# Second attention on 32-row and 32-column tiles of PE, conditioning weights rounded by ACT in the first attention

## The chip, the cores and the metric

One Trainium2 chip, one of its cores, one launch. The metric is the device time of one execution in microseconds. The core has five engines that run beside each other, each in its own program order, and wait for each other at semaphores: PE multiplies matrices, DVE (VectorE) and ACT (ScalarE) work element by element and read PE's results from PSUM (eight banks of 128 x 512 fp32), POOL (GpSimd) works on SBUF alone, SP issues transfers.

## The reference, cut to what matters

Four transformer blocks in a row on x of 4 batches x 256 tokens x 128 features, with a conditioning vector per batch:

```python
# layer 0: 16 heads of 64, then an MLP with gelu
qkv = mod(layernorm(x)) @ W_qkv; x += g1 * (softmax(q k^T / 8) v @ W_out + b_out); x += g2 * mlp(...)
# layer 1: rms norm modulated by a small net, rotary embedding, 16 heads of 8, gated MLP
n = ada_rmsnorm(x, c, w_norm1, t1_w1, ...); q, k = rope(n @ wq + bq), rope(n @ wk + bk)
x += softmax(q k^T / sqrt(8)) v @ wo + bo;  x += (gelu(n2 @ w_gate) * (n2 @ w_up)) @ w_down
# layer 2: every linear layer rounds its rows to 8 bits and its weights to -1, 0, 1
def weight_quant(w): s = 1 / clip(mean(|w|), 1e-5); return clip(round(w * s), -1, 1) / s
h = bitlinear(silu(c), wa0); h = hgrn_mlp(h, wa1, wa2); h = bitlinear(h, wa3) + ba3
params = bitlinear(rmsnorm(h) * wr, wa4) + ba4            # shift, scale, gate for the tokens
x = ...  (products with wi, wf, wg, wo, wm1, wm2 and a recurrent scan)
# layer 3: linear attention with 16 heads of 8
```

The change concerns the attention of layer 1 (the second attention) and the conditioning chain of layer 2, which depends on the condition alone: wa0, wa1, wa2, wa3, wa4 ("the conditioning layers").

## The kernel before, in words

Everything stays in SBUF. Tokens lie in eight tiles of 128; banks, semaphores and the order of each engine's instructions are written out by hand, so an engine waits wherever its next instruction waits, with all that is queued behind it.

*First attention* (layer 0): 32 pairs of heads, one pair a round. PE makes the scores of two heads on two 64-row tiles (`pair_scores`), projects queries, keys and values of the next batch (`unit`), transposes the normalised probabilities of the pair two rounds back (`turn0`) and multiplies the values of the pair three rounds back on two 64-column tiles (`pair_values`). DVE takes maxima (`top0`) and copies transposed probabilities (`take0`), ACT makes exponentials with their sums, POOL multiplies by the reciprocals.

Then ACT sums the absolute weights of wa4 (`weight_sums`), the small products for layer 1's and layer 3's scales follow, and layer 0's MLP. The other sums are made by ACT between its steps up to the start of the second attention. POOL rounds all of layer 2's weights during the second attention and after it (`whole_weights`), three steps for each.

*Preparation of layer 1:* products with Wqkv, rotation by DVE, then queries and keys are split into a high and a low part so that fp32r products stay exact: a head of 8 features has 32 rows of `qaT` and `kaT` (high, low, high, low against high, high, low, low). Four heads lie in the 128 rows of one group.

*Second attention:* 64 heads (4 batches x 16), one a round, in the loop `for i in range(NH + 3)`. Since four heads share the 128 rows, the keys of one head are copied into a buffer `kaM` that is zero in the other 96 rows (`masked_key`), by DVE for the first 16 and by ACT for the rest. In a round PE makes two score matmuls (`scores`), transposes the probabilities of the head two rounds back in four 128 x 128 pieces (`turn`), and multiplies the values of the head three rounds back in four matmuls of 96 columns (`values`; the trace records each fp32 matmul as two passes, so eight rows a head; fp32r matmuls and transposes are one pass each). DVE reduces the maxima of the head (`top`) and copies the transposed probabilities (`take`); every fourth round it normalises (`normalise`). ACT makes two exponentials of 128 x 256 with the maximum as bias, each with its sum.

The conditioning layers are woven into this loop (`weave`): each begins at the round that `WEAVE` gives it and takes one step a round: square (ACT), power (POOL), products and maxima of a row (DVE), rounding, transposes (PE), product (PE), result (ACT).

## Time and profile before

| | |
|---|---|
| median of 3 runs | 538.32 us (538.28 to 545.02) |
| the profiled execution | 538.68 us |
| its span | 536.9 us, 8122 instructions |
| busy: PE, DVE, ACT, POOL | 412.2, 370.8, 306.4, 193.6 us |
| mean granted clock of PE | 0.869 of full speed |

The span runs from the first to the last instruction of the profiled execution. An engine's busy time counts every moment in which one of its instructions runs. A row of the chain of waits names the work that the end of the kernel depended on at that moment. Times below are counted from the start of the span. The page cuts the span into 40 slices; PE's clock in tenths is 9 (full) in most of the first 28 and 5 in most of the last 12.

### The profile page before, as it was taken

To read this page: it belongs to the slowest core of one execution; us is meant where nothing else is said; L and a number is where in the kernel's file an instruction comes from. 1 tells how busy PE (TensorE), PEld (TensorE's weight loads), DVE (VectorE), ACT (ScalarE), POOL (GpSimd) and SP (SyncE) were. 2 spreads that over 40 slices of the span, in tenths; PEclk is the share of its full clock that TensorE was granted. 3 is DMA by queue.
4 is the path that set the end of the run, shared out by engine and by line. 5 is a ranking of instruction groups with operands and counts; after the bars stand their busy time and mean duration, and the time that the engine had idled before them with its cause. 6 is when DMAs were issued, how large, how long until landed. Compare 5 with 4: busy or idle time off the path is not lost.

```text
span 536.9 us, 8122 instructions
## 1 busy us (share of the span) xinstructions
PE 412.2 (77%) x2641; PEld 310.5 (58%) x2641; DVE 370.8 (69%) x904; ACT 306.4 (57%) x957; POOL 193.6 (36%) x189
## 2 busy tenths in 40 slices
PE   5989999999999678757898999899992531155564
PEld 5656566667576556447797899888451421004353
DVE  4456557557579334967996788877369459879794
ACT  1574654653666384686689788555731861275352
POOL 1043434433466220015585855300673022272101
PEclk9999999999999969797999799899997555555597
DMA  8930000000000000000000000000000000000001
GB/s 319 444 153 1 1 1 1 1 2 2 0 3 1 1 0 2 0 0 2 1 2 0 2 2 1 1 2 1 0 1 0 1 0 0 0 2 1 0 2 39
DMA packets 3842, 13.33 MB, mean 25 GB/s; under 512 B 372, under 2 KB 2420, under 8 KB 3284
## 3 DMA queue, kind: packets, MB, share of 16 engines
q1 hardware_dynamic: 3800, 12.80, 6.0%
q8 instruction: 22, 0.36, 0.3%
q14 instruction: 20, 0.16, 0.1%
HBM read 12.28 MB, written 0.52 MB: 24 GB/s over the span
## 4 chain that ended last, share of the span: by engine, by line
PE 54%; DVE 23%; ACT 9%; issue 7%; POOL 5%; DMA 1%; POOLq 0%; SPq 0%; ACTq 0%; DVEq 0%
PE bank L927 6%; PE bank L884 6%; PE bank L907 6%; PE bank L954 6%; PE bank L941 5%; PE bank L912 3%; DVE area L1313 3%; PE bank L870 3%; PE bank L969 3%; ACT tab_ L487 3%; DVE area L1316 2%; DVE tab_ L1313 2%; PE bank L861 2%; ACT big L487 2%; PE bank L1021 2%
## 5 line engine op out<-in xcount | busy, mean ns | idle before, releaser
L487 ACT ACTIVATE tab_<-bank,nmax 128x256 f32<-128x256 f32 x168 | 77.6, 468 | 40.6 <-DVE nmax L1457 31.5
L884 PE MATMUL bank<-vpad,xT 128*128 128x96 f32 x512 | 71.2, 285 | 6.6 <-DVE xT L1463 6.4
L884 PEld LDWEIGHTS bank<-vpad,xT 128*128 128x128 f32 x512 | 65.7, 201 | 10.1 <-DVE xT L1463 9.3
L487 ACT ACTIVATE area<-bank 128x512 f32<-128x512 f32 (+3 forms) x68 | 36.9, 549 | 56.9 <-PE bank L912 19.9
L396 POOL TENSOR_TENSOR big<-big,rrec 128x512 f32<-128x512 f32 x44 | 44.8, 1040 | 66.0 <-DVE rrec L1507 65.9
L1491 DVE TENSOR_REDUCE nmax<-bank 128x2 f32<-128x512 f32 x64 | 43.2, 677 | 32.0 <-PE bank L927 32.0
L1499 DVE COPY area<-bank 128x512 f32<-128x512 f32 x64 | 42.5, 684 | 14.6 <-PE bank L941 13.4
L1457 DVE TENSOR_REDUCE nmax<-bank 128x2 f32<-128x512 f32 x64 | 43.6, 681 | 11.8 <-PE bank L861 11.4
L487 ACT ACTIVATE big<-bank,nmax 128x256 f32<-128x256 f32 x88 | 40.6, 472 | 17.9 <-PE bank L907 10.6
L1463 DVE COPY xT<-bank 128x512 f32<-128x512 f32 x64 | 43.4, 678 | 1.9 <-PE bank L870 1.5
L870 PE MATMUL bank<-tabs,tab_ 128*128 128x128 f32 x256 | 41.1, 286 | 0.0
L861 PE MATMUL bank<-kaM,qaT 128*128 128x256 f32 x128 | 32.8, 340 | 6.9 <-ACT tab_ L487 5.6
L907 PE MATMUL bank<-xT,w0s 128*128 128x256 f32 x128 | 33.9, 396 | 4.4 <-issue 4.4
L927 PE MATMUL bank<-area 64*128 64x256 f32 x256 | 36.3, 402 | 0.0
L1182 PE MATMUL bank<-identb,area 128*128 128x128 bf16 x40 | 6.0, 310 | 38.1 <-DVE area L1316 38.0
L954 PE MATMUL bank<-area 128*64 128x256 f32 x256 | 34.7, 392 | 0.6 <-ACT big L487 0.6
L424 POOL TENSOR_SCALAR area<-area 128x4 f32<-128x4 f32 x14 | 3.9, 276 | 85.9 <-ACT tab_ L487 54.8
L487 ACT ACTIVATION_READ_ACCUMULATOR tab_<-bank,nmax 128x1 f32 x168 | 33.1, 197 | 0.0
L442 POOL TENSOR_SCALAR w2s<-w2s 128x768 f32<-128x768 f32 (+4 forms) x15 | 32.5, 2169 | 1.2
L487 ACT ACTIVATE big<-bank 128x256 f32<-128x256 f32 (+1 forms) x41 | 17.7, 434 | 25.2 <-PE bank L954 16.3
L870 PEld LDWEIGHTS bank<-tabs,tab_ 128*128 128x128 f32 x256 | 31.6, 147 | 0.0
L927 PEld LDWEIGHTS bank<-area 64*128 64x128 f32 x256 | 22.0, 186 | 14.2 <-issue 12.8
(224 smaller groups left out, 909.4 us busy)
## 6 DMA issues: line engine op xcount, KB each, us to landing
w2s<-w SPq DMA_DIRECT2D x1, 4352.0 KB, 26.8
rows<-row SPq DMA_DIRECT2D x1, 1600.0 KB, 10.9
w0s<-w SPq DMA_DIRECT2D x3, 512.0 KB, 6.8
w1s<-w SPq DMA_DIRECT2D x1, 1408.0 KB, 15.8
w0s<-w SPq DMA_DIRECT2D x1, 1024.0 KB, 12.9
xs<-x SPq DMA_DIRECT2D x1, 512.0 KB, 4.3
out<-tab_ SPq DMA_DIRECT2D x2, 256.0 KB, 2.3
tabs<-tab SPq DMA_DIRECT2D x1, 421.5 KB, 5.2
```

Source lines behind the costliest of these rows:

```text
L396: pool.tensor_tensor(prob[n % SLOTS], prob[n % SLOTS], rrec0[:, n % 4, :].unsqueeze(2).to_broadcast([P, QT, SEQ]), ALU.mult).then_inc(S("a ...
L487: return nc.scalar.activation(o, i, f, **kw)
L861: m = mm(bank[half][:, q * SEQ:(q + 1) * SEQ], queries(q), keys, start=True, stop=True)
L870: m = nc.tensor.transpose(bank[2 + half][:, k * SEQ + q * P:k * SEQ + (q + 1) * P], A.prob[:, slot, q, k * P:(k + 1) * P], ident)
L884: m = mm(bank[4 + gslot][:, o:o + v(k).shape[1]], A.pT[:, half, k, q * P:(q + 1) * P], v(k), start=(k == 0), stop=(k == QT - 1))
L907: m = mm(to[:, cc * SEQ:(cc + 1) * SEQ], part(w0s, W0, "qkv", at, at + P), rhs, start=True, stop=True)
L927: m = mm(bank[(2 * p + a) % 4][:, q * SEQ:(q + 1) * SEQ], qT[r, b % 2, c, q * P:(q + 1) * P], kT[r, b % 2, c, :], start=True, stop=True)
L954: m = mm(bank[6][a * DH0:(a + 1) * DH0, 0:SEQ], vs[:, b % 2, k, c * P + a * DH0:c * P + (a + 1) * DH0], pT[:, (2 * p + a) % 4, k, :], star ...
L1457: V.tensor_reduce(nmax[:, half, :], bank[half][:, :].rearrange("p (q k) -> p q k", q=QT), AX, ALU.max, negate=True).then_inc(S(A.tag + "_m ...
L1463: V.tensor_copy(A.pT[:, half, :, :].rearrange("p k q -> p (k q)"), bank[2 + half][:, :]).then_inc(S(A.tag + "_pT"), 1)
L1491: V.tensor_reduce(nmax0[:, n % 4, :], bank[n % 4][:, :].rearrange("p (q k) -> p q k", q=QT), AX, ALU.max, negate=True).then_inc(S("a0_max" ...
L1499: V.tensor_copy(pT[:, n % 4].rearrange("p k q -> p (k q)"), bank[4 + n % 2][:, :]).then_inc(S("a0_pT"), 1)
```

## The change

*Second attention.* The zero-padded key copies, the transposes of the probabilities, their copies and the sums in ACT go. The scores are now computed twice, in two orientations, both on 32-row tiles: once with queries along the partitions, only for the maxima (`scores1`), and once with keys along the partitions (`shifted_scores`), so that the exponential is written in the orientation that the value product needs. Two heads are worked on at a time, in the order 0, 2, 4, 6, 1, 3, 5, 7 of eight, so that the two lie in different row tiles. The maxima of eight heads are split into a high and a low part (`maxima`, DVE), turned by PE, copied by ACT and added to the second scores by a matmul with a selecting matrix `picks`. The exponential is one activation of 512 a head. The values are padded to 32 columns with a one behind the eight features, so that one product gives values and sums; four heads go to four 32-column tiles of one bank (`values1`). They come out with features along the partitions and are turned back once a batch (`turn_values`), then normalised.

Scores run 12 rounds ahead of their second computation (`LEAD`), the values lag 18, and the loop has 90 rounds, two at a time. Four banks are a ring that scores, maxima, turned values and the conditioning products enter in one fixed order; three banks hold the second scores, one the values.

*Weights.* The absolute sums are made by DVE in rounds 5 to 11 of the first attention, added up by one matmul in round 12, and the conditioning weights are rounded by ACT in 20 pieces in rounds 14 to 27 (`rounds` and `signs`: scale and add a large number, then the sign of what is left), in place. POOL rounds only layer 2's token weights, between the steps of the conditioning layers. POOL's clearing of the value buffer waits for the last normed batch of the first attention. A result of the conditioning layers is taken one round earlier (RESULT 9 becomes 8).

```diff
-            def core_exp(A, n, slot, half, gslot, hg, g=None):
-                act.wait_ge(S(A.tag + "_max"), n + 1)
-                act.wait_ge(S(A.tag + "_T"), n + 1)
-                for q in range(QT):
-                    e = acti(A.prob[:, slot, q, :], bank[half][:, q * SEQ:(q + 1) * SEQ], ACT.Exp,
-                             bias=nmax[:, half, q:q + 1], accum_out=rsum[:, gslot, q, hg:hg + 1])
+            def exponents1(n):
+                act.wait_ge(S("a1_Z"), n + 1)
+                if n >= 8:
+                    act.wait_ge(S("a1_PV"), (n - 8) // 4 + 1)
+                acti(pT1[:, n % 8].rearrange("p k q -> p (k q)"), bank[4 + n % 3][:, :], ACT.Exp
+                     ).then_inc(S("a1_exp"), 1)
...
+            def scores1(n):
+                to = [ring_enter("S", x, 0) for x in (n, n + 1)]
+                for q in range(QT):
+                    for x in (n, n + 1):
+                        r, g, at = group_of(x)
+                        m = mm(to[x - n][:, q * SEQ:(q + 1) * SEQ], qaT[r, g, at + q * P:at + (q + 1) * P],
+                               kaT[r, g, at:at + SEQ], start=True, stop=True)
...
+            def shifted_scores(n):
+                if n % 8 == 0:
+                    pe.wait_ge(S("a1_M"), n // 8 + 1)
+                if n >= 2:
+                    pe.wait_ge(S("a1_exp"), n - 1)
+                for x in (n, n + 1):
+                    r, g, at = group_of(x)
+                    mm(bank[4 + x % 3][:, :].rearrange("p (k q) -> p k q", k=QT), picks[r, g, :],
+                       mrow[r, x // 8 % 2, :].unsqueeze(1).to_broadcast([32, QT, SEQ]), start=True, stop=False)
+                for k in range(QT):
+                    for x in (n, n + 1):
+                        r, g, at = group_of(x)
+                        m = mm(bank[4 + x % 3][:, k * SEQ:(k + 1) * SEQ], kaT[r, g, at + k * P:at + (k + 1) * P],
+                               qaT[r, g, at:at + SEQ], start=False, stop=(k == QT - 1))
+            def values1(u, k):
...
+                for n in range(4 * u, 4 * u + 4):
+                    h = head_of(n)
+                    j, low = h % 8 // 2, h % 2
+                    at = 16 + ((b * QT + k) * H + h) * 32 - 16 * low
+                    m = mm(bank[7][32 * j:32 * j + 32, part_ * SEQ:(part_ + 1) * SEQ], vpad[:, at:at + 32],
+                           pT1[:, n % 8, k, :], start=(low == 0 and k == 0), stop=(low == 1 and k == QT - 1))
...
+            for i in range(0, ROUNDS, 2):
                 if i < NH:
+                    scores1(i)
+                if i % 8 == M_LAG % 8 and 0 <= i - M_LAG < NH:
+                    turn_maxima((i - M_LAG) // 8)
...
                 weave(i)
+                weave(i + 1)
+                if 0 <= i - PV_LAG < NH:
+                    values1((i - PV_LAG) // 4, (i - PV_LAG) // 2 % 2)
+                if LEAD <= i < NH + LEAD:
+                    shifted_scores(i - LEAD)
...
-                acti(into[0:r, 0:src.shape[1]], src, ACT.Abs, accum_out=wsum[0:r, j:j + 1]).then_inc(S("wsum"), 1)
+                acti(rounded_at[u % 2][0:r, 0:n], src, ACT.Identity, scale=wscale[0:r, j:j + 1], bias=magic[0:r, 0:1]
+                     ).then_inc(S("wq_round"), 1)
...
+                acti((wa2q if name == "wa2" else w2q)[:, 2 * (lo + (0 if name == "wa2" else W2[name][0])):][:, 0:n],
+                     rounded_at[u % 2][0:r, 0:n], ACT.Sign, bias=magic[0:r, 1:2]).then_inc(S("wq"), 1)
...
-            pool.memset(kaM[:, :, :].bitcast(F32), 0.0).then_inc(S("kaM_zero"), 1)
+            pool.wait_ge(S("a0_normed"), NB)
+            pool.memset(vpad[:, :], 0.0).then_inc(S("v_zero"), 1)
```

PE in the middle of the second attention, three heads before (names: `bank` is PSUM, then the two operands):

```order
L861 MATMUL bank<-kaM,qaT 128x256 x2
L870 MATMUL bank<-tabs,tab_ 128x128 x4
L884 MATMUL bank<-vpad,xT 128x96 x4
L861 MATMUL bank<-kaM,qaT 128x256 x2
L870 MATMUL bank<-tabs,tab_ 128x128 x4
L884 MATMUL bank<-vpad,xT 128x96 x4
```

and in the changed kernel at the same place, where the rows from one L1157 to the next are two heads:

```order
L1157 MATMUL bank<-kaT,qaT 128x256 x4
L1199 MATMUL bank<-big,vpad 32x256 x4
L1178 MATMUL bank<-mrow,picks 128x512 x2
L1183 MATMUL bank<-qaT,kaT 128x256 x4
L1157 MATMUL bank<-kaT,qaT 128x256 x4
L1167 MATMUL bank<-tabs,w0s 128x128 x2
L1199 MATMUL bank<-big,vpad 32x256 x4
L1178 MATMUL bank<-mrow,picks 128x512 x2
```

Two heads are 14 instructions where they were 20, and none of them is a transpose, apart from the two for the maxima of eight heads (L1167).

DVE at the first step of the third conditioning layer before, where L1457 is the reduction of the maxima and L1463 the copy of the transposed probabilities:

```order
L1457 TENSOR_REDUCE nmax<-bank 128x2
L1463 COPY xT<-bank 128x512
L1313 TENSOR_TENSOR big<-big 4x576
L1457 TENSOR_REDUCE nmax<-bank 128x2
L1463 COPY xT<-bank 128x512
L1668 SCALAR_TENSOR_TENSOR big<-big,a4s,adrs 4x576
```

and now:

```order
L1561 TENSOR_REDUCE nmax<-bank 128x2 x2
L1414 TENSOR_TENSOR w0s<-w0s 4x576
L1561 TENSOR_REDUCE nmax<-bank 128x2
L1810 SCALAR_TENSOR_TENSOR w0s<-w0s,a4s,adrs 4x576
L1561 TENSOR_REDUCE nmax<-bank 128x2
```

The copies are gone and the conditioning steps stand among half as many operations as before.

ACT in round 15 of the first attention, where it gets two pieces of weights; before:

```order
L487 ACTIVATE area<-bank 128x512
L487 ACTIVATE big,rsum<-bank,nmax 128x256 x4
L487 ACTIVATE big<-bank 128x256
```

and now:

```order
L531 ACTIVATE area<-bank 128x512
L531 ACTIVATE big,rsum<-bank,nmax 128x256 x2
L531 ACTIVATE tab_<-w2s,magic,wscale 128x384 x2
L531 ACTIVATE big,rsum<-bank,nmax 128x256 x2
L531 ACTIVATE w2s<-tab_,magic 128x384 x2
L531 ACTIVATE big<-bank 128x256
```

Four activations stand between and behind the exponentials of the pair.

## Rows read from the trace of the kernel before

**Rows 1.** The page, part 4: the chain that ended last, by engine.

```profile
PE 54%; DVE 23%; ACT 9%; issue 7%; POOL 5%; DMA 1%; POOLq 0%; SPq 0%; ACTq 0%; DVEq 0%
```

**Rows 2.** Stages: length, busy us of each engine (instructions), PE clock, DMA.

```profile
14.00:173.00 159.00, 151.25 (x978) 101.79 (x976) 100.03 (x201) 90.15 (x314) 63.18 (x64) 1.00 0.12 50
...
254.00:372.00 118.00, 110.21 (x879) 102.89 (x880) 98.20 (x220) 85.68 (x297) 57.68 (x41) 0.96 0.01 1
...
440.00:505.00 65.00, 20.87 (x109) 10.41 (x110) 57.36 (x171) 26.53 (x82) 24.61 (x30) 0.50 0.00 1
```

**Rows 3.** The same view, the second attention and its first stretch at half clock.

```profile
239.10:374.10 135.00, 121.59 (x947) 113.55 (x947) 112.15 (x245) 97.49 (x335) 64.67 (x45) 0.94 0.01 1
...
242.40:249.20 6.80, 6.03 (x28) 5.97 (x29) 4.45 (x9) 5.55 (x23) 2.27 (x4) 0.50 0.01 4
```

**Rows 4.** Timeline (start us, us, what, idle before): both ends of the second attention.

```profile
237.98 1.09 ACT L487 ACTIVATE kaT<-bank 128x512 fp32r<-128x512 f32 x2 [0.32 <-PE bank L1065]
...
374.12 0.66 PE L1103 MATMUL bank<-tabs,xn 128*128 128x128 f32 x4 [0.63 <-DVE xn L1313]
```

**Rows 5.** Chain of waits in order of time (start, us): one head.

```profile
280.65 0.27 PE bank L861 x2
280.91 0.44 PE bank L870 x4
281.35 0.87 PE bank L884 x8
```

**Rows 6.** Chain of waits, first attention: 16 fp32 matmuls (32 passes) of 256 columns.

```profile
14.50 7.14 PE bank L907 x32
```

**Rows 7.** Timeline of PE, first attention: one round with no projections.

```profile
145.66 1.14 PE L927 MATMUL bank<-area 64*128 64x256 f32 x8
...
146.72 1.09 PE L941 MATMUL bank<-tabs,big 128*128 128x128 f32 x8
...
147.75 1.08 PE L954 MATMUL bank<-area 128*64 128x256 f32 x8
```

**Rows 8.** Groups of DVE, 239.1 to 374.1 us (busy us, mean ns, idle before).

```profile
L1457 DVE TENSOR_REDUCE nmax<-bank 128x2 f32<-128x512 f32 x64 | 43.6, 681 | 11.8 <-PE bank L861 11.4
...
L1463 DVE COPY xT<-bank 128x512 f32<-128x512 f32 x64 | 43.4, 678 | 1.9 <-PE bank L870 1.5
...
L1641 DVE CAST kaM<-kaT 32x256 fp32r<-32x256 f32 x16 | 8.3, 520 | 4.2 <-ACT kaT L487 3.7
...
L1313 DVE TENSOR_TENSOR xn<-bank,rrec 128x32 f32<-128x32 f32 x32 | 4.6, 185 | 0.5
```

**Rows 9.** Groups of ACT in the same stretch.

```profile
L487 ACT ACTIVATE tab_<-bank,nmax 128x256 f32<-128x256 f32 x128 | 59.2, 466 | 32.0 <-DVE nmax L1457 31.5
...
L487 ACT ACTIVATE kaM<-kaT 32x256 fp32r<-32x256 f32 x48 | 19.7, 410 | 0.9
...
L487 ACT ACTIVATE big<-bank,a4s 4x384 f32<-4x384 f32 x5 | 2.8, 568 | 0.1
...
L487 ACT ACTIVATE big<-bank 128x512 f32<-128x512 f32 x1 | 0.6, 593 | 0.0
```

**Rows 10.** Stages, columns as in rows 2: rounds 15 and 24 of the first attention.

```profile
99.79:103.80 4.01, 4.01 (x29) 2.40 (x28) 2.64 (x5) 2.69 (x13) 2.04 (x2) 1.00 0.01 2
...
145.70:148.80 3.10, 3.10 (x28) 2.03 (x26) 1.98 (x5) 2.12 (x10) 1.13 (x3) 1.00 0.00 0
```

**Rows 11.** Timeline between the attentions.

```profile
184.93 4.04 ACT L487 ACTIVATE big<-w2s 128x4608 bf16<-128x4608 f32 x1 [4.03 <-PE bank L969]
...
188.01 3.69 DVE L1316 TENSOR_SCALAR xn<-xs,mv,rstd 128x128 f32<-128x128 f32 x2 [0.81 <-POOL rstd L402]
...
188.04 3.51 POOL L411 MEMSET kaM<- 128x4096 f32 x1
...
193.43 1.95 PE L852 MATMUL bank<-tabs,xn 128*128 128x128 f32 x8
...
195.69 6.54 PE L1030 MATMUL bank<-xT,w0s 128*128 128x512 f32 x12 [0.32 <-ACT xT L487]
```

More of the change, by code:

```diff
@@ L557, in _ @@
                     exponents(2 * s)
+                for u in pieces_of(s):
+                    rounds(u)
                 for i in units[1:2]:
@@ L561, in _ @@
                     exponents(2 * s + 1)
+                for u in pieces_of(s):
+                    signs(u)
                 for i in units[2:]:
```

475 lines of the change are left out of this document (279 added, 196 removed).

## The prediction

> **What bounds the kernel now.** I read the chain of waits first. It gives PE 54% of the span and DVE 23% [rows 1], so I went on to the stages. In the first attention PE is busy 151.3 of 159.0 us at the full clock; in the second it is busy 110.2 of 118.0 us at a granted clock of 0.96, and DVE is busy 98.2 us of the same stretch [rows 2]. The whole second attention, from the last piece of the transposed keys at 239.1 us to the turn of its last outputs at 374.1 us, takes 135.0 us [rows 3, 4]. That is a quarter of the kernel, and nearly all of the change lies in it.
>
> What sets that stage is PE's work for one head. In a run without stalls the eight value passes take 0.87 us (four fp32 matmuls, each recorded as two passes), the two scores 0.27 and the four transposes 0.44, together 1.58 us [rows 5]. Sixty-four heads are 101 us of the 135. The other 34 are the start, the conditioning products woven in, waits of the three engines for each other, and stretches at half clock, of which the first runs from 242.4 to 249.2 us [rows 3]. A change that only shortened one of DVE's or ACT's operations would be hidden here; this one takes away PE work.
>
> **The second attention, change part by part.** The sum is made against the profiled execution, 538.7 us (span 536.9), which is 0.4 us above the median of 538.32.
>
> *PE.* Transposes (4 a head) go, and so do the value matmuls that load 128x128 weights for 96 columns. A pair of heads now costs four score matmuls, two of 512 columns that add the maxima, four transposed scores, and four fp32 value matmuls of 32 output partitions. Prices: an fp32r matmul of 256 columns is one pass and costs 0.135 us (two in 0.27 [rows 5]); an fp32 one is two passes of 0.223, 0.45 us alone (16 matmuls, 32 passes, in 7.14 [rows 6]); two on 64-row tiles or on 64-column tiles cost what one costs, since eight passes start-to-start take 1.06 and 1.01 us and not 1.78 [rows 7]. Loads of weights share in no row: eight 128-column ones take 0.87 us, 0.109 each [rows 5]. The trace has no 32-row or 32-column tile. Bounds for the ten fp32r matmuls of a pair: all in twos, 0.81; ten weight loads one after another, 1.09; no sharing, 1.62. I take 1.2, near the middle one, because the 64-row tiles share and the loads don't. Values: 0.45 us if four column tiles run together, 0.89 if two do, as now, 1.78 if none does; I take 0.5. Each round changes between kinds of tile twice. Eight 64-row passes as four pairs would be 4 x 0.223 = 0.89 and take 1.06 [rows 7], so a change costs about 0.17 us, two 0.34. Sum: 2.04 us, against 3.16 now. The turns of maxima (two transposes and a change for eight heads) and of values, and the woven products (25 passes and 15 small transposes, some 7 us), add about 0.36 a pair: **2.4 us.**
>
> The Trainium skill speaks against this layout on one point: "TensorEngine Tiling (Array Packing)", section Key Properties, says that changing the tiling mode drains TensorE. The trace agrees, the 0.17 us above being what such a change costs here. Without it the pair would be 2.06 us, with it 2.4.
>
> *DVE.* It keeps one reduction a head and loses the copy of the turned probabilities (43.4 us), the key casts (8.3 us) and most of the normalising [rows 8]. Durations overlap a little: DVE was busy 112.2 us [rows 3] while the rows of the stage add up to about 122, so I scale by 0.91: 0.62 us a reduction. The conditioning layers' small operations are what is left of the 112.2 after the two big groups, the casts, the normalising, its 16 reciprocals of 0.19 and the residual (2 x 0.69): about 17 us. They stay. New: eight times two small operations for the maxima (0.2 us each, like the 128x32 ones [rows 8], 3 us), four normalisings of about 0.6 us (2.4). So from the thirteenth head on DVE owes per pair 1.24 + 22.4/26 = 2.1 us. **PE stays the bound, with DVE close behind.**
>
> *ACT.* Two exponentials of 256 with accumulated sums and a key copy of 0.41 (mean, 48 of them) become one exponential of 512. An evacuation of 512 from PSUM is 0.593 us [rows 9], so a pair is 1.1 to 1.2 us. ACT is not the bound.
>
> *The stage in rounds.* The program runs the exponential 12 heads behind the scores, so there is a head and a tail. Rounds 0 to 11, reductions only: 12 x 0.62 and 1.1 for the first maxima and the first score, 8.5 us. Rounds 12 to 63: 26 pairs x 2.4 = 62.5 us. Rounds 64 to 75, no reductions left: six pairs, each of which waits on three banks. PE may write a pair only after the exponential two heads back, so a period is PE's six matmuls (0.65 to 0.8), two hand-overs (0.3) and one exponential (0.6), 1.65 us, 10 us in all. Last values, copy, four transposes, normalising: 3.5 us. That is 84.5 us without waits. Before, waits, weaving, cold clock and start made 34 us over PE's per-head work. The weaving and the start are in my sum already and POOL has less to do between two steps of a conditioning layer, so I take 8 of the 34. The stage becomes **92.5 us, 42.5 us less**. The bounds of this term are 0 and 34 us: 84.5 and 118.5.
>
> **The other stages.** *First attention, +3 us.* DVE gets 14 sums of weights in rounds 5 to 11 (0.2 to 1.3 us by their width), where PE needs more than twice the time of these sums for its own round; that is hidden. ACT gets 20 pieces of two activations of 384. A 384-wide one with a pointer scale on 4 rows is 0.568 us [rows 9]; two with overlap are about 1.07 us. In round 15 ACT is busy 2.69 of 4.01 us [rows 10] and gets two pieces, 4.8 us: 0.8 too much. Round 24 has 2.12 of 3.10 and gets one, 3.2: 0.1 too much; six or seven rounds are like these two, most others have room. Taken together 1.5 to 2 us, and as much again for exponentials that come later to POOL. Bounds 0 and 8 us. If the cover in rounds 14 to 27 were gone altogether the 20 pieces would cost 21 us.
>
> *Between the attentions, -5 us.* ACT's sum of 4608 weights (4.04 us) stood ahead of the table load and the small conditioning matmuls, so PE turned the normed rows only at 193.43 [rows 11]. Now those matmuls follow the first attention directly and are done near 187. What is late next is DVE's normed batch: its two operations took 3.69 us because POOL's memset of 3.51 us ran beside them [rows 11]. POOL now waits for that batch before it clears the value buffer, so the batch ends near 188.5 and the first hidden layer starts near 190.1 instead of 195.69. The memset then runs beside the small operations that make the scales, and PE's fifth hidden matmul waits for these. I take 5 of the 5.6 us; bounds 3 and 7, the upper one if the clock no longer falls. The Trainium skill names such a mechanism ("GPSIMD Engine Reference", section Key points: GpSimd shares its SBUF interfaces with VectorE); the row with 3.69 us agrees.
>
> *Preparation and tail, -0.5.* One more DVE operation (a cast of 512 elements, 0.5 to 1 us) stands ahead of the DVE-bound rotation; the three key casts ahead of the first score go, 0.5 us. POOL's rounding of weights behind the second attention delayed nothing but some 0.5 us.
>
> 538.7 + 3 - 5 - 42.5 - 0.5 = 493.7, or 493.3 on the scale of the median: **493 us**.
>
> **Rivals.**
> 1. *The three engines keep waiting for each other as before.* Rounds are shorter, but a conditioning layer still needs eight hand-overs, two table switches and POOL's power, and ring banks used for its products make the next scores wait for ACT. Then the stage is 118.5 us and the time 519. For it: the 34 us of today. Against it: POOL's 768-wide roundings are gone.
> 2. *Column tiles run by twos at most*, as in the rows. A pair is 0.39 dearer: 8.5 + 26 x 2.8 + 12 + 3.5 + 8 = 105, time 506. For it: [rows 7] show two. Against it: nothing there says that two is the limit.
> 3. *Half clock through the stage.* Two of four row groups work at a time. The last stages run at 0.50 with PE busy 20.9 of 65.0 us [rows 2]. PE's passes double and a pair is 4.4: 8.5 + 114 + 19 + 4 + 6 = 152, time 553. Against it: PE's queue would hardly be idle, and the stages with PE busy over 90% had 0.96 and 1.00.
> 4. *Slower than before: 32-wide tiles do not run side by side at all.* A pair is 1.62 + 1.78 + 0.34 + 0.36 = 4.1 us, the drain 3.6 a pair: 8.5 + 107 + 22 + 3.5 + 8 = 149, time 550. The point from which it decides, for this and for rival 3, is about 3.7 us a pair (26 of them and six of the drain at 0.5 less, with 20 us of ends and waits, fill the 137.5 us that would cancel the other gains). For it: no row has such tiles. Against it: both 64-wide kinds share.
> 5. *Row tiles share their loads too.* Then PE owes 0.81 + 0.5 + 0.34 + 0.36 = 2.0 and DVE's 2.1 is the bound: 8.5 + 55 + 10 + 3.5 + 2 = 79, time 480; with the best bounds elsewhere 475.
>
> **How the numbers follow.** Chances: forecast (483 to 503) 0.56, rival 1 0.10, rival 2 0.14, rival 3 0.06, rival 4 0.04, rival 5 0.10. A change under 2% (10.8 us) cannot be told from none; that limit is 527.6. The forecast and rivals 1, 2 and 5 lie clear of it: 0.89 faster. Cases between rival 1 and rivals 3 and 4 give 0.03 within; slower 0.08. The range runs from 476 to 519: it takes in rival 2, nearly all of rival 5 and half of rival 1.
>
> **What the next profile would show.** Right: about 92 us from the last key copy to the last turn; PE busy over 90% of it, most idle time of the 64 reductions put down to its scores; the first hidden layer near 190 us plus what the first attention grew; 32-row matmuls starting in twos a few ns apart. Wrong if: four 32-column passes take 0.45 us (rival 2) or 0.9 (4), the granted clock of the stage is under 0.7 (3), PE is idle over 20 us of it (1), or the rounds 15 to 27 of the first attention are 1 us longer each.

## The result, and the profile after

The changed kernel takes 521.5 us (median of 4 runs, 517.8 to 525.6) against 538.4 of the kernel before in the same job: 0.961 of it, 95% interval 0.953 to 0.969. It is faster by 17 us where 45 were forecast, and lies outside my range (476 to 519). The profiled execution took 520.65 us, its span is 518.9. Run again later, the same kernel took 529.0 us (520.7 to 532.1), 0.972 of before (0.961 to 0.983). A kernel's profile is that of its first run, which was among the slower ones of e4, e7, e13 and e16 below and the fastest of e6.

Part 2 of its page, the row of PE's clock (40 slices of the span, tenths of full speed), and part 4, the chain by engine:

```profile
PEclk9999999999999989877575555997895555555597
PE 57%; DVE 25%; ACT 7%; issue 7%; POOL 2%; DMA 1%; POOLq 0%; SPq 0%; ACTq 0%; DVEq 0%
```

Before, the clock was nearly all 9 up to slice 28. Now it is at 5 in slices 18 to 25, which is the second attention. The view by stretches says the same in numbers; its columns are those of [rows 2]:

```profile
14.00:172.50 158.50, 149.65 (x962) 100.82 (x962) 109.03 (x214) 108.79 (x349) 62.18 (x62) 1.00 0.12 50
238.50:352.00 113.50, 84.58 (x663) 47.87 (x663) 62.19 (x141) 53.74 (x112) 23.96 (x32) 0.65 0.00 1
238.50:248.80 10.30, 4.79 (x30) 3.12 (x30) 9.09 (x23) 2.59 (x7) 3.99 (x8) 0.64 0.00 0
248.80:336.80 88.00, 68.89 (x521) 39.06 (x521) 50.48 (x113) 41.63 (x83) 19.28 (x22) 0.60 0.00 1
268.90:327.00 58.10, 46.06 (x319) 25.46 (x317) 32.71 (x72) 21.67 (x46) 15.39 (x14) 0.50 0.00 1
327.00:352.00 25.00, 18.41 (x198) 9.95 (x190) 8.28 (x17) 15.15 (x35) 0.69 (x2) 1.00 0.00 1
336.80:348.20 11.40, 8.77 (x90) 4.45 (x90) 1.84 (x4) 7.75 (x15) 0.00 (x0) 1.00 0.01 1
352.00:372.00 20.00, 20.00 (x52) 10.28 (x51) 5.19 (x13) 10.85 (x26) 1.76 (x3) 0.74 0.00 1
```

The second row is the whole second attention. The turn of its last outputs starts at 351.60 us, 0.4 before the end of the row, so in the measure of [rows 3] and of my forecast (from the end of the last key copy to that start) it takes 113.1 us where it was 135.0 and where I had 92.5. The granted clock is 0.65 where it was 0.94, and for 58 us on end it is at the lower of its two levels. PE is idle for 28.9 of the 113.5 us. The third, fourth and seventh rows are rounds 0 to 11, 12 to 63 and 64 to 75. I had 8.5, 62.5 and 10 us for them, and 8 us of waits: nearly all of the miss is in the 88.0.

PE's timeline, one pair of heads at full and one at half clock (start, us, what, idle before):

```profile
262.21 0.50 PE L1178 MATMUL bank<-mrow,picks 32*128 32x512 f32 x2
262.55 0.39 PE L1183 MATMUL bank<-qaT,kaT 32*128 32x256 f32 x4
262.78 0.40 PE L1157 MATMUL bank<-kaT,qaT 32*128 32x256 f32 x4
263.11 0.64 PE L1199 MATMUL bank<-big,vpad 128*32 128x256 f32 x8
263.80 0.50 PE L1178 MATMUL bank<-mrow,picks 32*128 32x512 f32 x2
...
286.42 0.79 PE L1178 MATMUL bank<-mrow,picks 32*128 32x512 f32 x2
287.01 0.63 PE L1183 MATMUL bank<-qaT,kaT 32*128 32x256 f32 x4
287.45 0.62 PE L1157 MATMUL bank<-kaT,qaT 32*128 32x256 f32 x4
288.00 1.08 PE L1199 MATMUL bank<-big,vpad 128*32 128x256 f32 x8
289.01 0.79 PE L1178 MATMUL bank<-mrow,picks 32*128 32x512 f32 x2
```

From one L1178 to the next, a pair is 1.59 us at full clock and 2.59 at half. Every other pair is shorter where nothing is woven in. In these the first scores of a later pair (L1157) lie in the other two row tiles and start 0.02 us behind the selecting matmuls (L1178); from the L1178 to the next it is 1.43 us at full clock (333.99 to 335.42) and 2.16 at half:

```profile
302.63 0.79 PE L1178 MATMUL bank<-mrow,picks 32*128 32x512 f32 x2
302.65 0.79 PE L1157 MATMUL bank<-kaT,qaT 32*128 32x256 f32 x4
303.22 0.62 PE L1183 MATMUL bank<-qaT,kaT 32*128 32x256 f32 x4
303.77 1.08 PE L1199 MATMUL bank<-big,vpad 128*32 128x256 f32 x8
304.79 0.79 PE L1178 MATMUL bank<-mrow,picks 32*128 32x512 f32 x2
```

The answer to [rows 5] is a full-clock run of value passes in the chain, 16 passes in four column tiles:

```profile
348.24 1.11 PE bank L1199 x16
```

Who waited for whom in 238.5 to 352 us (us, times, longest):

```profile
ACT big L531 <- PE bank L1183: 48.6, 28, 5.8
DVE nmax L1561 <- PE bank L1157: 36.9, 16, 5.9
...
PE bank L1107 <- DVE w0s L1417: 8.5, 5, 3.5
...
PE bank L1210 <- ACT xT L531: 5.4, 4, 2.2
```

DVE and ACT wait for PE, and PE waits for DVE's clipped rows of a conditioning layer at its transposes (L1107), and for the copy of the values. The timeline between the attentions, which answers to [rows 11]:

```profile
182.65 3.81 PE L1000 MATMUL bank<-w0s,big 128*128 128x128 f32 x32 [0.52 <-issue]
...
189.66 0.60 DVE L1417 TENSOR_SCALAR xn<-xs,mv,rstd 128x128 f32<-128x128 f32 x2 [0.81 <-POOL rstd L461]
190.32 3.53 POOL L470 MEMSET vpad<- 128x4112 f32 x1 [0.70 <-DVE xn L1417]
190.46 1.94 PE L911 MATMUL bank<-tabs,xn 128*128 128x128 f32 x8 [1.65 <-DVEq L1718]
190.81 3.54 DVE L1417 TENSOR_SCALAR ada<-ada,cols 128x4 f32<-128x4 f32 x2
192.66 7.59 PE L1061 MATMUL bank<-xT,w0s 128*128 128x512 f32 x12 [0.26 <-ACT xT L531]
```

**The books.** The span went from 536.9 to 518.9: up to the last copy of the keys -0.6 us (239.1 to 238.5), the second attention -21.9, the rest +4.5 (162.8 to 167.3). Against the prediction, 493.7 for this execution, it is 27 us: 1.9, 20.6 and 4.5.

### The profile page after: what moved, and what is told of

The parts are those of the page before. It is cut to its first block, busy times and chain, and to the rows that moved or that the text cites. A ratio compares the mean times of both kernels' runs of the same rounds, so it can differ in the third digit from the quotient of the medians.

```text
span 518.9 us, 7080 instructions
## 1 busy us (share of the span) xinstructions
PE 381.3 (73%) x2352; PEld 247.3 (48%) x2353; DVE 331.3 (64%) x815; ACT 272.0 (52%) x748; POOL 136.4 (26%) x162
## 4 chain that ended last, share of the span: by engine, by line
PE 57%; DVE 25%; ACT 7%; issue 7%; POOL 2%; DMA 1%; POOLq 0%; SPq 0%; ACTq 0%; DVEq 0%
PE bank L954 7%; PE bank L934 6%; PE bank L981 6%; PE bank L968 5%; PE bank L939 3%; DVE area L1414 3%; DVE nmax L1561 3%; PE bank L1052 3%; PE bank L1000 3%; PE bank L1199 3%; DVE tab_ L1414 3%; DVE area L1417 3%; PE bank L1178 2%; ACT big L531 2%; PE bank L1268 2%
## 5 line engine op out<-in xcount | busy, mean ns | idle before, releaser
L531 ACT ACTIVATE big<-bank 128x512 f32<-128x512 f32 (+1 forms) x104 | 53.1, 530 | 70.0 <-PE bank L1183 48.6
L1561 DVE TENSOR_REDUCE nmax<-bank 128x2 f32<-128x512 f32 x64 | 42.3, 680 | 37.1 <-PE bank L1157 36.9
L1199 PE MATMUL bank<-big,vpad 128*32 128x256 f32 x256 | 30.2, 525 | 0.6 <-ACT big L531 0.6
L934 PEld LDWEIGHTS bank<-xT,w0s 128*128 128x128 f32 x128 | 22.3, 189 | 14.5 <-issue 12.5
L455 POOL TENSOR_TENSOR tab_<-tab_,rrec 128x512 f32<-128x512 f32 x20 | 20.4, 1042 | 21.8 <-DVE rrec L1616 21.8
L968 PE MATMUL bank<-tabs,big 128*128 128x128 f32 x176 | 25.3, 276 | 0.3 <-POOL big L455 0.2
L1178 PE MATMUL bank<-mrow,picks 32*128 32x512 f32 x64 | 21.7, 674 | 5.0 <-ACT big L531 3.9
L968 PEld LDWEIGHTS bank<-tabs,big 128*128 128x128 f32 x176 | 20.6, 141 | 8.9 <-issue 5.4
L1157 PE MATMUL bank<-kaT,qaT 32*128 32x256 f32 x128 | 20.6, 418 | 4.6 <-DVE nmax L1561 3.9
L489 POOL TENSOR_TENSOR area<-area,halves 128x4 f32<-128x4 f32 x22 | 22.8, 1035 | 1.8
L1283 PEld LDWEIGHTS bank<-identb,area 128*128 128x128 bf16 x40 | 4.0, 139 | 39.8 <-DVE area L1417 26.1
## 6 DMA issues: line engine op xcount, KB each, us to landing
w2s<-w SPq DMA_DIRECT2D x1, 4352.0 KB, 26.4
```

The source lines that it names most:

```text
L455: pool.tensor_tensor(prob[n % SLOTS], prob[n % SLOTS], rrec0[:, n % 4, :].unsqueeze(2).to_broadcast([P, QT, SEQ]), ALU.mult).then_inc(S("a ...
L531: return nc.scalar.activation(o, i, f, **kw)
L934: m = mm(to[:, cc * SEQ:(cc + 1) * SEQ], part(w0s, W0, "qkv", at, at + P), rhs, start=True, stop=True)
L968: m = nc.tensor.transpose(bank[4 + n % 2][:, k * SEQ + q * P:k * SEQ + (q + 1) * P], prob[n % SLOTS][:, q, k * P:(k + 1) * P], ident)
L1178: mm(bank[4 + x % 3][:, :].rearrange("p (k q) -> p k q", k=QT), picks[r, g, :], mrow[r, x // 8 % 2, :].unsqueeze(1).to_broadcast([32, QT, ...
L1199: m = mm(bank[7][32 * j:32 * j + 32, part_ * SEQ:(part_ + 1) * SEQ], vpad[:, at:at + 32], pT1[:, n % 8, k, :], start=(low == 0 and k == 0) ...
```

## Experiments

"Stage" is the time from the start of the last key copy to the start of the second turn of outputs in the profiled execution, with the granted clock in it (0.6 us more than when it is counted from the end of that copy). The kernel before had medians of 538.4 to 540.4 us in the jobs behind this table, and 545.1 (538.3 to 546.3) in that of e16; its stage is 135.6 us at 0.94. The changed kernel ran in the first job and in that of e5, e6 and e7 alone, so the others are compared with it across jobs.

| kernel | median, range (us) | stage, clock |
|---|---|---|
| changed kernel | 521.5, 517.8 to 525.6 | 113.7, 0.65 |
| changed kernel, again | 529.0, 520.7 to 532.1 | 118.7, 0.57 |
| e1_warm128 | 551.0, 548.1 to 555.3 | 141.0, 0.60 |
| e2_warm32 | 529.4, 525.2 to 532.8 | 121.9, 0.58 |
| e6_warm8 | 550.3, 538.1 to 572.0 | 130.1, 0.84 |
| e5_rows128 | 530.5, 526.4 to 531.2 | 125.4, 0.78 |
| e10_bursts | 528.0, 526.7 to 532.4 | 122.0, 0.73 |
| e8_no_layers | 507.8, 504.5 to 510.7 | 98.1, 0.54 |
| e9_turn_later | 520.1, 518.5 to 520.6 | 113.2, 0.58 |
| e11_later_start | 520.2, 518.1 to 520.9 | 111.6, 0.65 |
| e14_both_later | 517.5, 516.7 to 517.6 | 109.8, 0.56 |
| e12_values_bf16 | 522.1, 517.5 to 525.5 | 108.5, 0.56 |
| e15_both_later_bf16 | 515.5, 507.7 to 518.3 | 102.2, 0.52 |
| e3_no_pieces | 520.6, 520.4 to 522.7 | 118.8, 0.58 |
| e4_memset_early | 528.2, 522.8 to 535.7 | 118.7, 0.58 |
| e7_before_rows32 | 624.8, 585.3 to 625.1 | 221.5, 0.55 |
| e13_before_rows64 | 608.8, 586.8 to 631.4 | 220.3, 0.55 |
| e16_before_tiny32 | 579.0, 558.1 to 580.1 | 171.6, 0.79 |

### The clock: extra work on full rows

My first theory (A) was the clock alone: the array is mostly idle in narrow tiles, so give it full rows.

```diff
                 to = [ring_enter("S", x, 0) for x in (n, n + 1)]
+                for x in (n, n + 1):          # e2: rows r of head x in place of :
+                    r_, g_, at_ = group_of(x)
+                    for c_ in range(2):       # e6: 4
+                        mm(to[x - n][:, c_ * SEQ:(c_ + 1) * SEQ], kaT[:, g_, at_:at_ + P], qaT[:, g_, at_:at_ + SEQ],
+                           start=True, stop=True)
```

> The changed kernel with four more fp32r matmuls of 256 columns on all 128 rows for each pair of heads, written by PE into the two banks just before the first scores overwrite them (128 extra matmuls in all, nothing else changed; results unaffected). Theory A (the granted clock): the 21 us that the second attention takes more than forecast come from the half clock, which the chip grants because products on 32 of 128 rows or columns leave most of the array idle; 128-row products hold the clock. A pair of heads at full clock takes 1.73 us in the changed kernel's trace, with the four extra ones 1.73 + 0.54 = 2.3 us, against 2.6 to 3.4 at half clock: stage (last key copy to last turn) 92 to 97 us against 113.5, time 501 to 506, granted clock of the stage over 0.9. Theory B (the engines' waits set the pace, the clock only follows): the extra matmuls fill waits or lengthen the rounds: stage 113 to 131 us, time 521 to 538, and what clock is granted hardly matters.

> The same four extra matmuls for a pair, but on the 32 rows of the head whose bank they are written to. Theory A as stated (idle rows of the array bring the clock down): the clock stays at half, and the extra PE work at half clock costs 0.5 to 1.1 us a pair: stage 125 to 140 us, time 533 to 548. Theory A' (only the time in which PE works counts, not how much of the array): the clock comes back as with 128 rows, stage 92 to 97, time 501 to 506. Theory B: 521 to 538, as with 128 rows.

With 128 rows it was 551 us, above what either theory gave, and the clock of the stage stayed at 0.60: from 241 to 299 us it was at half although PE was busy nearly throughout. With 32 rows it was 529 us, at a clock of 0.58. The extra work bought nothing, so theory A as I had stated it fell (its time, not yet its cause), and also A', by which PE's busy time decides. The 529 us lie in the range of theory B, the 551 above it; what the waits cost is the matter of e8. What was left of A was that four matmuls were too few. Two kernels tried that:

```diff
-                        m = mm(to[x - n][...], qaT[r, g, at + q * P:at + (q + 1) * P], kaT[r, g, at:at + SEQ], ...)
+                        m = mm(to[x - n][...], qaT[:, g, at + q * P:at + (q + 1) * P], kaT[:, g, at:at + SEQ], ...)
```

(e5; the same in `shifted_scores`)

> The changed kernel with its eight score matmuls of a pair (both orientations) on all 128 rows instead of 32; every instruction, its columns and its bank stay, and so do the selecting matmuls on 32 rows. What is computed changes: a score is then the sum over the four heads that share the rows. With the four extra 128-row matmuls a pair, the clock had stayed at half although PE was busy without a gap; so theory A must now say that the share of the array at work over the whole pair counts, and that four extra ones were too few beside ten narrow ones. Theory A: all scores on full rows bring the clock to full for most of the stage; a pair is then 8 x 0.107 + 0.50 + 0.57 + changes, 2.1 us, DVE and PE even, stage 84 to 95 us, time 491 to 502. Theory C (row tiles have no part in it, the clock stays down for another reason, such as fp32r passes or waits): half clock stays, a pair is 8 x 0.213 + 0.72 + 1.01 = 3.5 us, stage 130 to 145 us, time 538 to 552.

> Eight extra 128-row matmuls of 256 columns a pair instead of four (256 in all). Theory A: now two thirds of PE's time in a pair is on the full array, the clock rises and a pair is 1.73 + 1.07 = 2.8 us: stage 98 to 105, time 505 to 513, faster than with four although PE does more. Theory C or B: the clock stays at half, a pair is 2.6 + 2 x 0.85 + changes = 4.5 us: stage 150 to 165, time 570 to 590.

Both raised the clock, to 0.78 and 0.84 of the stage, so the narrow tiles have to do with its staying down. Neither gained: 530 and 550 us, against 529 for the changed kernel in the same job, and neither time lies in a range on record. In e5 a pair takes 2.14 us at full clock and 3.74 at half (313.47 to 317.21 us), the changed kernel's 1.59 and 2.59, and the waits for the layers stayed (8.1 us at L1107). A full clock bought with PE work is paid for by that work.

### The clock, in the kernel before

```diff
-                    scores(A1, i, i % 2, lambda q: qaT[:, g, at + q * P:at + (q + 1) * P], kaM[:, i % H, :])
+                    r_ = slice(32 * (i % 4), 32 * (i % 4) + 32)      # e13: the 64 rows that hold them
+                    scores(A1, i, i % 2, lambda q: qaT[r_, g, at + q * P:at + (q + 1) * P], kaM[r_, i % H, :])
```

> The kernel before with its two score matmuls of a head on the head's own 32 rows (queries and masked keys; the result is the same), everything else as it was: 128 of its matmuls on 32 rows, no new waits. Theory A: the score products are 0.27 of 1.58 us of PE's time for a head, so the full clock is lost more often but not for good; two changes between kinds of tile a head cost up to 0.3 us: time 540 to 560. Theory C: nothing but the changes of tile, 64 x 0.1 to 0.3 = 6 to 19 us, at a granted clock of the stage as before (0.94).

> The kernel before with its two score matmuls of a head on 64 rows (the half of the rows in which the head lies; the masked keys are zero in the other 32, so the result is the same). With 32 rows the kernel before took 625 us and its second attention stayed at half clock. If any row tile (or the change between kinds of tile) keeps the clock from coming back, it is 585 to 625 us again. If it is the small share of the array, 64 rows lie between: the clock comes back in places, 545 to 590 us. If 64 rows do no harm, as in the first attention, which runs at full clock with them: 540 to 555 us, the changes of tile alone.

Neither theory had this: three runs at 625 us with a mean clock of 0.74, and one at 585 with 0.80. Two of a head's fourteen passes go to 32 rows, and the second attention is 86 us longer. With 64 rows two runs took 628 and 631 us and two 587 and 589, the first outcome on record. Stretches of e7's stage (columns as in [rows 2]):

```profile
244.00:430.00 186.00, 185.50 (x765) 161.76 (x765) 100.97 (x202) 83.96 (x288) 63.99 (x45) 0.50 0.00 1
239.00:460.50 221.50, 216.27 (x947) 187.37 (x947) 120.05 (x245) 99.14 (x337) 63.99 (x45) 0.55 0.00 1
```

PE is busy 185.5 of 186 us and the clock stays at its lower level all that time. So busy time alone does not decide whether the clock comes back. It did so at 444.7 us, and in e13 at 440.9, in both during six products of the last conditioning layer on 128 rows; no run tests whether these bring it back. The first attention has 64-row tiles too, and keeps the full clock that it enters with. To tell the narrow work from the changes between kinds of tile, e16 has the changes with next to no narrow work:

```diff
                 pe.wait_ge(S(A.tag + "_exp"), n + 1)
+                mm(bank[half][:, 0:4], kaT[0:32, 0, 0:P], qaT[0:32, 0, 0:4], start=True, stop=True)
                 for q in range(QT):
```

> The kernel before with one more matmul a head, of 4 columns on 32 rows, ahead of its two scores, which are on 128 rows again (64 extra matmuls; it is overwritten, the result is the same). PE's work on few rows is next to nothing now, the two changes between kinds of tile a head are as with the 32-row scores. If the changes of kind keep the clock down, the second attention is at half clock for most of its length and the time is 585 to 640 us. If the work on few rows does, the clock is that of the kernel before (0.94 in this stage) and only the changes cost, 64 x 0.1 to 0.35 us: 545 to 562 us.

It came out between the two, and its profile shows why:

```profile
243.00:314.00 71.00, 70.17 (x297) 65.46 (x297) 40.41 (x81) 31.26 (x114) 33.47 (x19) 0.50 0.00 1
315.00:410.00 95.00, 91.31 (x707) 83.31 (x705) 72.72 (x155) 62.54 (x214) 31.08 (x26) 1.00 0.01 1
```

The same loop runs 71 us at half clock and then 95 us at full. Work that holds the clock need not bring it back. It fell at 243 us, in the thin start of the second attention, as in the kernel before, which had it back 7 us later [rows 3]; here it took 71. Its four runs (580, 580, 578, 558 us) fit a clock that returns at another moment each time. The changes of tile with next to no narrow work are enough to delay it (to 314.5 us), and with narrow scores it came back later still in the profiled runs (440.9 and 444.7). One run of e7 took 585 us, near e16's 580, so how much each of the two weighs, and what exactly the chip counts, the runs leave open.

### Bursts where PE waits

```diff
+            def full_rows(to, n):
+                for c in range(n):
+                    mm(to[:, c % 2 * SEQ:(c % 2 + 1) * SEQ], kaT[:, 0, 0:P], qaT[:, 0, 0:SEQ], start=True, stop=True)
...
                 to = ring_enter("AT", ADA_NAMES.index(name), 0)
+                full_rows(to, 16)                             # e10
...
+                if n < LEAD:                                  # e10, and e11 on top of e9
+                    for x in (n, n + 1):
+                        full_rows(to[x - n], 4)
```

> The changed kernel with extra 128-row matmuls only where PE waits anyway: four for each head in rounds 0 to 11 (DVE sets their pace) and 16 ahead of each layer's transposes, 128 in all. Theory A in the form that the runs so far leave (the clock falls in a stretch with little PE work, and rises only after a stretch in which nearly all of it is on full rows, so that it has to be kept from falling): the clock does not fall at 241 us and at the layers' waits, or comes back in rounds 0 to 11; granted clock of the stage over 0.8, stage 95 to 105 us, time 503 to 514. If it falls all the same, the extra work is at half clock and costs up to 5 x 3 us: stage 115 to 130, time 523 to 538.

> The layers' transposes two rounds later, and four extra 128-row matmuls a head in rounds 0 to 11 alone. With theories A and D both right this has the full clock up to the first long wait and fewer such waits: time 505 to 515. If the clock is lost again in rounds 12 to 30, it is that of the layers' transposes moved alone, within 3 us.

In e10 the clock held up to 254 us instead of 241 and came back three times, 0.73 in the stage, yet the time was 528, the dear case of its expectation: a burst of 16 at half clock takes 3.78 us, and the waits that they stood in had been 8.5 us in five. In e11 the clock fell at 252 us, and the time is that of e9, the second outcome on record.

### The waits: conditioning layers out, or later

> The changed kernel without the five conditioning layers in the second attention (none of their squares, powers, products, transposes and roundings; layer 2's scale, shift and gate are the raw parameter rows). In the changed kernel a pair of heads takes 2.59 us at half clock and 1.42 to 1.6 at full where nothing is woven in, but the 31 gaps between pairs add up to 97.5 us, with gaps of 4 to 7 us where layers stand. Theory D (two costs add: the waits for the layers' steps on DVE and ACT, some 25 us, and the half clock, some 20 us): without the layers the waits go and the stage is 31 x 2.6 + 10 + 5 = 90 to 96 us at half clock, less if the clock comes back; time 496 to 503. Theory A alone (only the clock matters): a PE that waits less has no more reason for full clock, the layers' own PE work of some 7 us goes, and the stage is 105 to 110 us, time 511 to 518.

(e8 drops `weave` on PE, ACT and DVE, POOL's powers, and the layers' places in the ring.) The stage fell to 98.1 us and the time to 507.8. Theory D (two costs add) had 90 to 96 and 496 to 503, the clock alone 105 to 110 and 511 to 518: the stage is near D's, the time lies between the two. Rounds 12 to 63 alone, to be held against the 88.0 us above:

```profile
248.60:319.40 70.80, 67.60 (x486) 37.54 (x486) 37.87 (x72) 32.06 (x62) 0.00 (x0) 0.52 0.00 1
```

At a clock of 0.52 the 26 pairs take 70.8 us, 2.72 each, and PE is busy 67.6 of them. So the five layers are 17 us of these rounds, nearly all of it PE's idle time (19.1 us of the 88.0 at a clock of 0.60, 3.2 of the 70.8 at 0.52), and what is left is PE at half clock. How they cost it shows in the changed kernel's chain of waits, the third layer (start, us):

```profile
269.80 0.81 DVE w0s L1810
270.60 0.60 DVE nmax L1561
271.20 0.66 DVE a4s L1814
271.86 0.60 DVE nmax L1561
...
273.00 0.60 DVE nmax L1561
273.60 0.43 DVE w0s L1417
...
274.56 0.99 DVE w0s L1417
...
275.59 0.48 PE bank L1107 x4
```

Between POOL's power, done at 269.7, and PE's transposes at 275.6 DVE has twelve operations, eight small ones of the layer and four reductions of scores, and PE has waited 3.5 us at the end of them.

```diff
-        WEAVE = {"wa0": 2, "wa1": 12, "wa2": 25, "wa3": 35, "wr": 47, "wa4": 49}
+        WEAVE = {"wa0": 2, "wa1": 14, "wa2": 29, "wa3": 41, "wr": 55, "wa4": 57}
-        USE, TOP, WORTH, SCALE, CLIP, TURN, TAKE, PRODUCT, RESULT = 1, 2, 3, 4, 5, 6, 7, 8, 8
+        USE, TOP, WORTH, SCALE, CLIP, TURN, TAKE, PRODUCT, RESULT = 1, 2, 3, 4, 5, 8, 9, 10, 10
```

> The changed kernel with each layer's transposes on PE two rounds later (step 8 instead of 6, and the steps behind it; the layers start 2 to 8 rounds later in turn). PE waits 8.5 us in all for DVE's clipped rows at its transposes of a layer (five times, 3.5 us at most). Theory D: one pair more in between gives DVE the time, these waits shrink to under 3 us and the time falls by 4 to 7 us, to 514 to 522 on a chip where the changed kernel takes 521 to 529. Rival: DVE is late because it is the bound around the layers' steps; the wait only moves from the transposes to the ring of scores, time within 2 us.

> The changed kernel with the layers' transposes two rounds later on PE, and the turn of a batch's values two rounds later as well (the copy by ACT stays where it is). The first alone gave 1 to 2 us. PE waits 5.4 us in all for ACT's copy of the values (four times). If waits add up as theory D has it, another 2 to 4 us: time 514 to 519. If these waits are only exchanged for the ones behind, the time is that of the first alone, 518 to 521.

(e14 also turns a batch's values at `F_LAG` 36 on PE while ACT copies them where it did.) In both PE no longer waits for DVE's rows at the transposes (8.5 us in the changed kernel). PE's idle time in the stage falls from 29.6 us (26.4 in the second profile of the changed kernel) to 21.2 and 17.2, but the clock is 0.58 and 0.56 in it against 0.65 (0.57), so little of that reaches the time. e9 is 520.1 us, e14 517.5 with four runs within 0.9 us, 0.958 of before (0.954 to 0.961). The ratios of the changed kernel were 0.961 and 0.972, so e14 is some 2 to 8 us ahead, but the intervals touch, and no job had both. It changes no result and is the version I would keep.

### Fewer passes for the values

> The changed kernel with the exponentials and the padded values kept in bf16, so that the value product of a pair is four passes instead of eight (it is computed less exactly; nothing else changes). If PE at half clock sets the pace between the waits, a pair goes from 2.59 to about 2.15 us (eight passes in four column tiles take 0.85 us at half clock, four take 0.43): stage 10 to 14 us shorter, time 508 to 516. If the waits for the layers and for DVE's reductions set it, or the clock falls oftener with less work, the time moves by under 4 us.

> Both moves and the bf16 values together. If the passes and the waits are separate terms: 503 to 510 us. If shorter pairs at half clock only bring the waits for DVE and ACT back: 508 to 516 us.

(`pT1` and `vpad` in bf16.) Half the value passes took 5 to 10 us off the stage of the kernel they were put into (118.7 or 113.7 to 108.5, and 109.8 to 102.2), but e12's time did not move. It was given back right behind the stage: there, on full tiles, the clock stayed down longer.

```profile
346.20:376.00 29.80, 29.79 (x78) 15.89 (x78) 6.57 (x15) 11.65 (x27) 1.71 (x3) 0.64 0.00 1
```

The same 30 us behind the stage are at 0.83 in the changed kernel's profile and at 1.00 in that of the kernel before. e15 with 515.5 us (ratio 0.946, 0.937 to 0.955) has the second outcome on record. Of the kernels that leave no work out it has the lowest median, with less exact values.

### The two small terms

```diff
-                for u in pieces_of(s):
-                    rounds(u)
+                    act.sem_inc(S("wq_round"), 1)      # e3; signs(u) likewise, products take a constant
...
-            pool.wait_ge(S("a0_normed"), NB)           # e4
```

> The changed kernel without ACT's 40 activations that round the conditioning weights in the first attention; the conditioning products take a constant instead of these weights. The prediction priced them at 3 us of the first attention (bounds 0 and 8). If that is right the last output product of the first attention starts 2 to 3 us earlier (182.65 us in the changed kernel), and the time falls by 2 to 3 us, to 518 to 520, unless the second attention loses or gains with a clock that falls at other places. A rival: the slip is DVE's sums of weights; then it stays and the time is that of the changed kernel within 1 us.

> The changed kernel with POOL's clearing of the value buffer no longer waiting for the last normed batch of the first attention (as before the change). The step of the prediction: this wait is worth 2.5 to 3 us, since DVE's normed batch then runs beside the 3.5 us clearing. Expected: the normed batch on DVE takes 3.6 instead of 0.60 us, the first hidden layer starts 2.5 to 3 us later than 192.66 us, time 523 to 525. Rival: the clearing runs beside the small conditioning operations on DVE in both kernels (3.54 us for one of 0.2 us), so that it only changes its victim and the time stays within 1 us.

```profile
181.53 3.81 PE L1001 MATMUL bank<-w0s,big 128*128 128x128 f32 x32 [0.52 <-issue]
```

Without the pieces (e3) the last output products of the first attention start at 181.53 us instead of 182.65 and 183.17: the pieces cost 1.1 to 1.6 us where 2 to 3 were expected. Without POOL's wait (e4):

```profile
190.06 4.04 DVE L1416 TENSOR_SCALAR xn<-xs,mv,rstd 128x128 f32<-128x128 f32 x2 [0.81 <-POOL rstd L461]
...
196.51 3.69 PE L1060 MATMUL bank<-xT,w0s 128*128 128x512 f32 x6 [0.26 <-ACT xT L530]
```

The normed batch takes 4.04 us instead of 0.60 and the first hidden layer starts 3.4 to 3.9 us later than in the two profiles of the changed kernel (192.66 and 193.13). Counted from each kernel's last output products, the start is 13.5 us behind them in e4 (183.05 to 196.51) and 10.0 in both profiles of the changed kernel. The wait is worth 3.5 us at that place, a little more than the 2.5 to 3 of the expectation. In both kernels the whole time hangs on the clock in the second attention (522.8 to 535.7 in e4), which is wider than either term.

## Why the prediction was wrong

**The step that failed** is in the third rival: half clock through the stage, chance 0.06, with "PE's queue would hardly be idle, and the stages with PE busy over 90% had 0.96 and 1.00" against it. I took the clock for a function of PE's busy time. Of those two stages the one at 0.96 had 128 rows for every head, the one at 1.00 had 64-row tiles but entered with the full clock, and the rows could not show what narrower tiles do. The stage ran at 0.65, between my forecast and that rival. The rival's own price (152 us, 4.4 a pair) was too high, because a pair costs less than I thought at either clock. The sign of rival 1 (PE idle over 20 us) came true as well, with 28.9 us idle, and its 118.5 us are the nearest of all the stages that I had priced. It had the waits but not the clock: by e8 the waits are about 16 us of the stage, twice the 8 of my sum. That its time of 519 is so near the measured one is luck.

**PE's price for a pair** was mis-sized in the other direction. It is 1.59 us at full clock (1.43 where four row tiles work at a time), not 2.4. From the first L1178 to the values are 0.90 us with the ten fp32r matmuls and one change of tile (I had 1.2 and 0.17): row tiles do share their loads, which was rival 5 (chance 0.10). The eight value passes with the change behind them are 0.69 (0.67 expected): 16 passes in 1.11 us confirm four column tiles side by side. That is 0.45 us below the 2.04 of my sum without the woven work, and the 0.36 for that had no business in a price per pair: it comes in lumps, with waits. The Trainium skill says under "TensorEngine Tiling (Array Packing)", section Key Properties, that tiles load weights and multiply in parallel. The 0.90 us agree, and I had held the loads of [rows 5], all of full width, against it.

**Rounds 12 to 63**, 88.0 us against 62.5 and 8 of waits. By e8 they are 70.8 us without layers, at a clock of 0.52. So 17 us are the layers, and PE's idle time alone accounts for 16 of them, twice the 8 that I had for all waits. The rest is 2.72 us a pair against my 2.4. I had written that the weaving is in my sum already. Its PE work was; PE's wait behind twelve DVE operations in their written order was not.

**DVE and ACT** were right: a reduction comes every 0.60 us in the chain (0.62), an exponential of 512 is 0.59. Neither is the bound; DVE waits 36.9 us for PE's scores, in 16 waits.

**Start, drain, end**: 10.3, 11.4 and 3.4 us against 8.5, 10 and 3.5. In the first DVE sets the pace, PE is busy 4.79 us, and there the clock falls.

**First attention** +2.1 us against +3 (it began 0.44 us earlier and its last products came 1.65 later), of which the pieces are 1.1 to 1.6. **Between the attentions**: the hidden layer starts at 192.66, 3.0 us earlier than before, although the last products came 1.65 later. That is a gain of 4.7 us where I had 5, for the reason given (e4). What I did not follow was the clock. It comes back at 197.1 us now and came back at 198.0 before, so the first twelve matmuls of that layer have 4.4 us of half clock instead of 2.3 and take 7.59 us instead of 6.54. In the second profile of the changed kernel they have 1.3 us of it and take 6.07. POOL's clearing, which now holds DVE's small operation for 3.54 us, is not the reason: it does so there too, for 3.55. **The rest**, behind the second attention, lost 4.5 us where I had next to nothing: the clock is 0.74 in 352 to 372 us, and was 1.00 in the same 20 us behind the stage before.

**How large the clock's part is.** Eight runs of the changed kernel lie between 517.8 us at a mean clock of 0.801 and 532.1 at 0.767. The difference of 0.034 over some 525 us is 36 us more at half clock, for 14.3 us of time: 0.4 us for each. At that rate the 79 us that the stage is at half clock (0.35 x 2 x 113.5) would be some 30 us. That is an estimate that goes more than twice as far as the runs differ: DVE's 2.1 us a pair would stop it sooner, and no kernel here had the narrow tiles and the full clock together through the stage (the changed kernel had them for 6.8 us from 261.9 on and for its last 25). What is shown is that PE at half clock is the bound of the pairs (e8), that narrow tiles, or the changes to them, delay the clock's return (e5, e7, e13, e16), and that the layers' waits are a second term beside it (e8).

## What to carry to other kernels

Before PE work is moved to narrow tiles, ask in which state of the clock the stage is entered and what will bring the clock back after its first thin stretch; price the stage at both levels, and what stands behind it too. A chain of small steps woven into a loop costs its waits in lumps, however short its instructions: count what stands in the queue of the engine that is waited for, and give the waiting engine a pair or two of other work in between. Extra PE work for the clock's sake won nothing in any of five kernels (e1, e2, e6, e10, e11).

## What the runs showed of the hardware

- The granted clock has a memory: the same loop ran 71 us at 0.50 and then 95 us at 1.00 (e16). PE was busy 185.5 of 186 us at 0.50, and the clock was back only 201 us after it fell (e7, 243.3 to 444.7 us). The Trainium skill says under "TensorE: Matmul & The Clock Gate", Part 1, that the gate follows how busy PE has been. By that rule the clock would have been back early in e7, and its time what its expectation had without a lost clock, under 560 us. Three runs had 625: with narrow tiles in the loop busy time is not the measure.
- Two matmuls of different row tiles start together and their loads overlap: at full clock the eight score matmuls from 262.55 to 263.11 us take 0.56 us with one change of tile behind them, four pairs of 0.11 (four matmuls in 0.23, 262.55 to 262.78) and some 0.1 for the change (0.17 expected). Four row tiles work at a time too: L1157 starts at 302.65 beside L1178 at 302.63.
- POOL's memset of 3.5 us can hold a DVE operation that runs beside it until it is through: two of 128x128 took 3.69 us before and 4.04 in e4 (0.60 without it), two of 128x4 took 3.54 (0.50 without it). Not every operation is held: the two DVE additions that read PSUM (`ada<-bank,cols`) took 0.37 us at 190.41, beside the memset of 190.32, and 0.37 before without one.
